# Routing tokens to experts group by group, later second norms, reordered gathers and first keys in two parts

## The chip, the cores and the metric

One core of a Trainium2 chip runs the whole program. The metric is the device time of one execution in microseconds. Three runs of the kernel before gave 1108.84 to 1109.99, median 1109.43. The engines named below: TensorE (PE, with weight loads as PEld), VectorE (DVE), ScalarE (ACT), GpSimd (POOL), SyncE (SP, which here only issues DMAs).

## What is computed

32 sequences of 128 tokens with 192 features pass an embedding, two attention layers and a layer of experts. Cut to what matters here:

```python
emb = word_table[ids] + domain_table[dom] @ proj_w.T + type_table[0] + pos_table[pos]
h = norm(emb) * gamma + beta
h = h + softmax(|complex scores|) @ v            # layer 1, of norm(h): "mag"
x = norm(h)                                      # layer 2: "cau", causal softmax
x = x + attention(norm(x) * w1 + b1)
z = norm(x) * w2 + b2
logits = z @ w_g                                 # 4096 tokens, 8 experts
_, topk_idx = top_k(logits, 2)
hot = one_hot(topk_idx)                          # first choices of all tokens, then second
exp_rank = cumsum(exp_mask.reshape(2 * N, 8), axis=0) - 1   # place in the expert
exp_mask = exp_mask * (exp_rank < cap)           # cap = 1280 slots of each expert
out = gelu(xb @ fc_w + fc_b) @ pj_w + pj_b       # xb: the tokens of an expert's slots
y = weights of the two choices * out, added up;  result h + x + y
```

The weights of the two choices are a softmax over two logits.

## The kernel before, in words

**Groups and passes.** The sequences go in 8 groups of 4. Each group has 12 jobs (4 sequences by 3 blocks of heads) in each of the two layers; numbers 0 to 7 are the groups of the first layer (`mag`), 8 to 15 those of the second (`cau`). Every engine runs the same written schedule: a loop over passes -2 to 17, of 16 slots each. In pass p the scores of number p are made, the transposes of probabilities and the products with the values belong to number p - 1, the embedding norms on POOL to p + 2 and the gathers to p + 3. What TensorE makes for others in a slot is a fill: it goes to one of three ring banks in PSUM, in the order that `fills_of` (line 118) lists, which PE, ACT and DVE all follow. Within a slot the engines do their parts in one fixed order, so a late item on an engine holds everything behind it there.

**Steps of a causal group after its scores.** `LAGS` (line 86) gives the slot of each step, counted from the start of the pass after the scores, for sequence s three slots later each: the context is transposed at 5, transposed again at 7, multiplied by the output weights at 9; POOL makes the scale of the norm at 10, DVE normalises z at 12 (`normalise_z`, 1345), PE transposes z at 13 (`zT`), ACT scales it, PE makes the logits at 15, and DVE takes the best two (1339 to 1343). The last group, number 15, has its own shorter `LAST_LAGS`.

**Gathers and embedding norms (POOL).** In a pass POOL issues, for group p + 3, four gathers of words in slots 0 to 3, four of places in slots 4 to 7 that add to them, and four of domains in slots 8 to 11 (`gather_step`, 577). For group p + 2 it makes two reciprocal square roots (`embedding_norm`, 612; `power`, 564): for groups 0 and 1 in slots 4 and 6, for the others in slots 4 and 12. Each waits for moments that DVE makes, and DVE waits for the result at `embedding_step` (1440). POOL does these in order of slots.

**First keys.** In the first layer DVE writes the keys of each of the three blocks to `k` and, with signs, to `k_signed` (1293 to 1299), and SP moves them to other partitions with eight DMAs. For group 0 SP waits for all three blocks and sends them at once (474 to 478); for the other groups it sends block after block (484). TensorE waits for the moved keys before its first scores.

**Routing.** After the last pass DVE (`route_tokens`, 1572) subtracts the two best logits, marks the choices of all 4096 tokens in `hot`, PE sums them over partitions and DVE over tiles (scans at 1596), and the rank of each of the 64 pairs of tile and choice follows. A slot number is split in a low part of 7 bits and a high one. For 16 batches of four pairs DVE marks both (1624, 1627), ACT multiplies the high marks with the token's number (1185) and PE adds up a table of 128 by 80 slots (942). DVE turns it into `slot_src` and `slot_dst` (1634 to 1642). The weights of all tokens go to memory in one DMA (522) behind the rows of z, and SP then loads the expert weights `pj_w` and `fc_w` (510, 505). POOL (`move_rows`, 642) waits for the table, the rows and the weights and gathers each expert's rows (624); the experts follow. `low_hot` and `high_hot` of the routing lie where the experts' rows come later, `number` in `work`.

The two waits at which POOL stands before the experts' first rows:

```python
                pool.wait_ge(map_ready, 1)
                slots_at_hand(0, slot_src, 0, 0, src_copied)
                pool.wait_ge(rows_stored, 2 * 16 * GROUPS)
                pool.wait_ge(weights_stored, 16)
                for t in range(CAP_TILES):
                    take_row(0, t)
```

## Time and profile before

| | |
|---|---|
| median of 3 runs | 1109.43 us |
| the profiled execution | 1110.32 us |
| its span, first to last instruction | 1107.4 us |
| mean granted TensorE clock | 0.916 |
| TensorE busy | 947.6 us, 86% |
| VectorE busy | 666.7 us, 60% |
| ScalarE busy | 676.9 us, 61% |
| GpSimd busy | 458.7 us, 41% |
| chain that ended last | PE 64%, DVE 14%, ACT 7%, issue 6%, POOL 3%, SP 3%, DMA 2% |

The busy share is a mean over stages that differ. In the timeline a row gives the start, the length, the engine, the line of the kernel, what is written and read, and in brackets how long the engine had been idle and what ended that.

### The profile page before, as it was taken

The numbers are of one execution on the slowest core, as the hardware profiler recorded it, in microseconds if no ns is written. First come the engines' busy times: TensorE is split into PE (matmuls) and PEld (weight loads), VectorE is DVE, ScalarE is ACT, GpSimd is POOL, SyncE is SP. The second block draws the span as 40 slices with busy tenths as digits, with TensorE's granted clock in tenths as the row PEclk, the third lists the DMA queues.
The fourth block names the chain that finished last, engine by engine and source line by source line (L and its number), as shares of the span: only waits on it lengthen the run. The fifth ranks groups of instructions, "written<-read, shape, count | busy, mean of one in ns | idle before, by whom it ended". The sixth has DMA issues, their size and how long they took to land.

```text
span 1107.4 us, 22074 instructions
## 1 busy us (share of the span) xinstructions
PE 947.6 (86%) x7209; PEld 724.2 (65%) x7210; DVE 666.7 (60%) x3063; ACT 676.9 (61%) x1438; POOL 458.7 (41%) x508
## 2 busy tenths in 40 slices
PE   2477778988988889999899989856999999999996
PEld 1444555565655566666666666545888888889896
DVE  1576778878988776767677665483443443443432
ACT  2148768958888978788778777354444443443431
POOL 7765547533110111222322122203667667567654
PEclk7668889989999999999999998656999999999999
DMA  7333223212011000011101101145454445564342
GB/s 212 66 50 59 45 54 72 38 41 47 13 24 48 13 2 1 2 35 35 34 2 35 35 18 48 34 85 70 74 106 84 79 104 79 76 111 78 50 52 28
DMA packets 63236, 59.24 MB, mean 53 GB/s; under 512 B 17278, under 2 KB 54176, under 8 KB 63136
## 3 DMA queue, kind: packets, MB, share of 16 engines
q0 software_dynamic: 25344, 27.89, 17.7%
q1 hardware_dynamic: 37792, 30.11, 10.6%
q8 instruction: 51, 0.84, 0.3%
q14 instruction: 49, 0.40, 0.1%
HBM read 35.28 MB, written 16.39 MB: 47 GB/s over the span
## 4 chain that ended last, share of the span: by engine, by line
PE 64%; DVE 14%; ACT 7%; issue 6%; POOL 3%; SPq 3%; DMA 2%; POOLq 0%; DVEq 0%; ACTq 0%
PE ps_scores L759 13%; PE ps_ring L751 11%; PE ps_ring L1003 9%; PE ps_ring L759 7%; PE ps_scores L877 5%; PE ps_ctx L894 5%; PE ps_scores L1003 4%; PE ps_scores L880 3%; SPq L484 2%; POOL got L573 2%; DVE probs L1377 2%; PE ps_ring L831 1%; PE ps_ring L830 1%; DMA k<-k_signed 1%; ACT square L1101 1%
## 5 line engine op out<-in xcount | busy, mean ns | idle before, releaser
L1214 ACT ACTIVATE probs<-ps_scores,fc_bias 128x512 f32<-128x512 f32 (+1 forms) x144 | 87.9, 616 | 148.6 <-PE ps_scores L759 143.7
L633 POOL DMA_INDIRECT out<-z_t,slots_now x80 | 135.2, 1690 | 103.6 <-DVE z_t L1688 73.8
L1092 ACT ACTIVATE prob_t<-ps_ring 128x512 f32<-128x512 f32 x192 | 114.1, 597 | 39.4 <-PE ps_ring L751 38.7
L751 PE MATMUL ps_ring<-ident,probs 128*128 128x128 f32 x768 | 127.8, 292 | 6.6 <-ACT k L1072 1.9
L1117 ACT ACTIVATE probs<-probs,neg_max 128x128 f32<-128x128 f32 x384 | 120.6, 395 | 3.5 <-DVE neg_max L1377 3.5
L1101 ACT ACTIVATE square<-ps_scores 128x512 f32<-128x512 f32 x192 | 104.8, 601 | 29.0 <-PE ps_scores L877 25.3
L1377 DVE CUSTOM_DVE_ANT_0 probs<-ps_scores,causal 128x128 f32<-128x128 f32 x384 | 88.8, 287 | 53.1 <-PE ps_scores L880 52.8
L1003 PE MATMUL ps_ring<-work,probs 128*128 128x192 f32 x672 | 115.9, 328 | 5.7 <-ACT probs L1214 5.4
L1003 PEld LDWEIGHTS ps_ring<-work,probs 128*128 128x128 f32 x672 | 109.2, 190 | 9.5 <-issue 9.5
L759 PE MATMUL ps_scores<-x_hi,fc_hi 128*128 128x512 f32 (+1 forms) x288 | 105.4, 372 | 7.3 <-DVE x_hi L1672 3.6
L1371 DVE CUSTOM_DVE_ANT_0 probs<-square 128x128 f32<-128x128 f32 x384 | 89.8, 288 | 35.3 <-ACT square L1101 32.0
L751 PEld LDWEIGHTS ps_ring<-ident,probs 128*128 128x128 f32 x768 | 91.9, 149 | 26.2 <-issue 12.7
L759 PE MATMUL ps_scores<-x_hi,fc_lo 128*128 128x512 f32 (+1 forms) x288 | 102.0, 360 | 0.0
L1669 DVE CAST x_hi<-x_full 128x512 fp32r<-128x512 f32 x40 | 18.2, 456 | 138.9 <-ACT x_full L1203 93.9
L877 PE MATMUL ps_scores<-k,q 32*128 32x256 f32 x768 | 92.3, 475 | 11.0 <-DMA k<-k_signed 5.6
L567 POOL TENSOR_SCALAR rstd<-moments 128x4 f32<-128x4 f32 x24 | 6.7, 281 | 212.0 <-DVE moments L1502 121.1
L759 PE MATMUL ps_ring<-x_hi,w_hi 128*128 128x512 f32 x160 | 71.8, 449 | 12.8 <-DVE k L1293 6.8
L567 POOL TENSOR_SCALAR rstd<-z_moments 128x1 f32<-128x1 f32 x32 | 7.3, 227 | 171.8 <-DVE z_moments L1335 171.8
L877 PEld LDWEIGHTS ps_scores<-k,q 32*128 32x128 f32 x768 | 45.8, 204 | 36.5 <-issue 24.6
L759 PEld LDWEIGHTS ps_scores<-x_hi,fc_hi 128*128 128x128 f32 x288 | 55.1, 191 | 18.7 <-issue 6.7
L759 PE MATMUL ps_ring<-x_hi,w_lo 128*128 128x512 f32 x160 | 65.5, 409 | 0.0
L751 PE MATMUL ps_ring<-ident,xn 128*128 128x128 f32 x160 | 29.5, 316 | 41.7 <-DVE xn L1438 31.8
(215 smaller groups left out, 2199.1 us busy)
## 6 DMA issues: line engine op xcount, KB each, us to landing
k<-k_signed SPq DMA_DIRECT2D x168, 32.0 KB
work<-pj_w SPq DMA_DIRECT2D x8, 576.0 KB
token_in<-xin SPq DMA_DIRECT2D x8, 384.0 KB, 3.4
out<-resid SPq DMA_DIRECT2D x8, 384.0 KB, 4.2
vals<-fc_w SPq DMA_DIRECT2D x8, 384.0 KB
vals<-fc_w SPq DMA_DIRECT2D x16, 192.0 KB
out<-z_t,slots_now POOLq DMA_INDIRECT x80
token_in<-xin SPq DMA_DIRECT2D x8, 128.0 KB, 4.4
```

The lines of the kernel that those rows point to most:

```text
L633: gp.indirect_dma_start(out[:, :], bass.IndirectOffsetOnAxis(slots_now[:, u, 1, t:t + 1], 0), slot_y[:, o, :], None, compute_op=ALU.add).t ...
L751: return pe.transpose(dst, src, ident[0:n, 0:n])
L759: last = pe.matmul(dst, lhs, rhs, start=(k == 0), stop=(k == 4))
L877: last = pe.matmul(ps_scores[:, h, 0:256], q[r, b, s, :], k[r, b, :, s, :], start=True, stop=True)
L894: last = pe.matmul(ps_ctx[32 * h:32 * h + 32, 128 * b:128 * b + 128], vals_of[number % 2][:, s, 4 * b + h, :], prob_t[:, j % 2, h, :], sta ...
L1003: last = pe.matmul(ps_y[i][:, 0:HID], hidden[:, c % 2, f_, tok], pj_w_sb[:, u, f_, :], start=(f_ == 0), stop=(f_ == FF_CHUNKS - 1))
L1092: sc.activation(prob_t[:, s % 2, :, :], src.rearrange("p (h q) -> p h q", h=4), ACT.Exp if p is mag else ACT.Copy).then_inc(ring_free[i], 1)
L1101: sc.activation(square[:, j % 2, h, :, :].rearrange("p h m k -> p h (m k)"), ps_scores[:, h, 0:256], ACT.Square).then_inc(mag.scores_free, 1)
L1117: last = sc.activation(probs[:, j, h, :], probs[:, j, h, :], ACT.Exp, bias=neg_max[:, s, 4 * b + h:4 * b + h + 1], scale=-1.0)
L1214: sc.activation(hidden[:, c % 2, f_, 0:128 * nt], ps_scores[:, i, 0:128 * nt], ACT.Gelu, bias=fc_bias[:, e, f_:f_ + 1]).then_inc(gelu_done ...
L1371: last = ve.tensor_tensor_reduce(out=probs[:, j, h, :], in0=square[:, j % 2, h, 0, :], in1=square[:, j % 2, h, 1, :], scale=1.0, scalar=-3 ...
L1377: last = ve.tensor_tensor_reduce(out=probs[:, j, h, :], in0=ps_scores[:, h, 0:128], in1=causal[:, :], scale=-(HEAD_DIM ** -0.5), scalar=3. ...
```

## The change

- The routing of each causal group is done in pieces along with the passes: `mark_choices` in the last logits of a batch, a fill `rank` (place within the group by `below`, plus the sums of the tiles before), then on DVE `slots`, `low`, `high`, `parts`, `weights`, then a fill `map` whose result DVE adds to `slot_map`. The slots are given in `ROUTE`; for group 14 in `LATE_ROUTE`; the last group goes in two batches by `LAST_ROUTE`.
- First choices take an expert's slots from below, second choices from above, so neither needs the count of the other; at the end `used` strikes out second choices in tiles that do not count. Token numbers are sums of two bf16 products.
- The weights are stored group by group, by SP behind the rows of the group.
- `zT`, `keep` and `logits` come one slot later in all causal groups but the last.
- For groups 2 to 7 the first embedding norm on POOL moves from slot 4 to slot 8.
- In slot 1 of passes that follow a `mag` group TensorE does the other fills before the product with the values.
- The keys of group 0: block 0 goes as soon as it is signed; blocks 1 and 2 go half by SP and half by ACT, behind ACT's fourth projection.

```diff
+FIRST_Q = 3
-LAGS = {"ctx": 5, "ctxT": 7, "out": 9, "scale": 10, "norm": 12, "zT": 13, "keep": 13, "logits": 15}
+LAGS = {"ctx": 5, "ctxT": 7, "out": 9, "scale": 10, "norm": 12, "zT": 14, "keep": 14, "logits": 16}
+BATCHES = lambda number: ((0, 2), (2, 4)) if number == LAST else ((0, 4),)
+ROUTE = {"rank": 26, "weights": 27, "slots": 31, "low": 32, "high": 33, "parts": 34, "map": 35}
+LATE_ROUTE = {"rank": 26, "slots": 27, "low": 28, "high": 29, "parts": 30, "weights": 31, "map": 32}
+LAST_ROUTE = ({"rank": 18, "slots": 20, "low": 20, "high": 21, "parts": 21, "weights": 21},
+              {"rank": 23, "slots": 23, "low": 23, "high": 23, "parts": 23, "weights": 24, "map": 24})
...
+    fills += [f for f in route_due(number, at - STEPS) if f[0] in ("rank", "map")]
...
-    for away in (-1, -2, 0, 1, 2):
+    for away in (-1, -2, -3, 0, 1, 2):
...
@@ SP
+            sp.wait_ge(keys_signed, 1)
+            for quarter, part in product(range(4), range(2)):
+                turn_first_keys(sp, quarter, part, slice(0, 1), first_turned)
             sp.wait_ge(keys_signed, BLOCKS)
-            for quarter, part in product(range(4), range(2)):
...
+            for quarter, part in product(range(2), range(2)):
+                turn_first_keys(sp, quarter, part, slice(1, BLOCKS), rest_turned)
...
             with sp.Fori(0, GROUPS - 2, 1) as g:
                 store_rows(g)
+                store_weights(g)
...
-            sp.wait_ge(weights_made, 1)
+            store_rows(GROUPS - 2)
+            store_weights(GROUPS - 2)
+            store_rows(GROUPS - 1)
+            store_weights(GROUPS - 1)
             sp.wait_ge(cau.pv_done, JOBS * GROUPS + 2)
-            sp.wait_ge(hot_ready, 1)
+            sp.wait_ge(hot_ready, GROUPS + 1)
             load_second_layer(0)
@@ POOL
-                first, second = (4, 6) if g < 2 else (4, 12)
+                first, second = (4, 6) if g < 2 else (8, 12)
...
-                pool.wait_ge(weights_stored, 16)
+                pool.wait_ge(weights_stored, 16 * GROUPS)
...
+                if p == GROUPS - 1:
+                    count_up()
@@ PE
+                elif kind == "rank":
...
+                    pe.wait_ge(hot_ready, batch_no(number, s))
+                    tiles = lambda a, b: dst[:, width * (a - first):width * (b - first)]
+                    pe.matmul(tiles(first, end), below[:, :], hots[:, 1 + first:1 + end, :], start=True, stop=False,
+                              skip_group_check=True)
+                    for t in range(-1, end - 1):
+                        to = max(t + 1, first)
+                        last = pe.matmul(tiles(to, end), ones_b[:, :],
+                                         hots[:, 1 + t:2 + t, :].to_broadcast([128, end - to, width]),
+                                         start=False, stop=(t == end - 2), skip_group_check=True)
+                    if number == LAST and end == GROUP:
+
+                        for t in range(1 + GROUP):
+                            last = pe.matmul(dst[:, 256:256 + width], ones_b[:, :], hots[:, t, :],
+                                             start=(t == 0), stop=(t == GROUP), skip_group_check=True)
+                elif kind == "map":
+
+                    pe.wait_ge(lows_made, batch_no(number, s))
+                    pe.wait_ge(parts_made, batch_no(number, s))
+                    for k in range(TOPK):
+                        for t in range(GROUP):
+                            last = pe.matmul(dst[:, 2 * HIGH * k:2 * HIGH * (k + 1)], low_hot[:, TOPK * t + k, :],
...
-                        pe.wait_ge(first_turned, 8 * 16)
+                        pe.wait_ge(first_turned if j == 0 else rest_turned, 8 * 16)
...
+                    turned = ready is not None and ready < GROUPS and slot == 1
+                    if ready is not None and 1 <= slot <= JOBS and not turned:
                         values_product(ready, slot - 1)
                     for n, f in fills:
                         fill(n, f)
+                    if turned:
+                        values_product(ready, slot - 1)
@@ ACT
+                if kind == "rank":
+                    now, pairs, tt = tiles_of(number, s)
+                    act.wait_ge(gap_ready, batch_no(number, s))
+                    sc.activation(gap[:, 1, tt], gap[:, 0, tt], ACT.Exp).then_inc(gap_exp, 1)
...
+            def turn_rest_of_keys():
+
+                act.wait_ge(keys_signed, BLOCKS)
+                for quarter, part in product(range(2, 4), range(2)):
+                    turn_first_keys(act, quarter, part, slice(1, BLOCKS), rest_turned)
...
+                        if (n, f) == (0, ("proj", FIRST_Q)):
+                            turn_rest_of_keys()
@@ DVE
+                    for b, (first, end) in enumerate(BATCHES(number)):
+                        if s == end - 1:
+                            mark_choices(number, b)
...
+                    for away in (-1, -2, -3):
+                        n, at = group_of(p, away), slot - STEPS * (away + 1)
+                        if n is not None and n >= GROUPS:
+                            for what, b in route_due(n, at):
+                                route_piece(what, n, b)
...
+                    step(ve.tensor_scalar(at_low[:, pairs], slots, -(LOW - 1) / 2, TO_LOW, ALU.add, ALU.add))
+                    step(ve.tensor_scalar(at_high[:, pairs], at_low[:, pairs], -TO_LOW, None, ALU.add))
+                    ve.tensor_tensor(at_low[:, pairs], slots, at_high[:, pairs], ALU.subtract).then_inc(slots_made, 1)
+                elif what == "low":
+
+                    dve.wait_ge(slots_made, done)
+                    ve.tensor_tensor(low_hot[:, pairs, :], number.unsqueeze(1).to_broadcast([128, n_pairs, LOW]),
+                                     at_low[:, pairs].unsqueeze(2).to_broadcast([128, n_pairs, LOW]), ALU.is_equal
+                                     ).then_inc(lows_made, 1)
...
+                    ve.tensor_scalar(high_part[:, pairs, 0, :], high_hot[:, pairs, :], place_in, None, ALU.mult)
+                    for t in range(now.start, now.stop):
+                        two = slice(TOPK * t, TOPK * t + TOPK)
+                        last = ve.tensor_scalar(high_part[:, two, 1, :], high_hot[:, two, :],
+                                                128.0 * (GROUP * (no - GROUPS) + t), None, ALU.mult)
...
             def route_tokens():
...
+                dve.wait_ge(map_added, GROUPS)
                 second, token, empty = (of_slot[:, i, :] for i in range(3))
...
+                ve.tensor_tensor(first, first, slot_map[:, 0, 1, :], ALU.add)
+                step(ve.tensor_tensor(second, slot_map[:, 1, 0, :], slot_map[:, 1, 1, :], ALU.add))
+                step(ve.tensor_tensor(second, second, used[:, :], ALU.mult))
+                step(ve.tensor_tensor(token, second, first, ALU.add))
```

## Rows read from the trace of the kernel before

**Rows 1.** Windows: us, busy (instructions) by engine, PEclk, DMA share, GB/s

```profile
534.20:541.10 6.90, 6.07 (x62) 4.30 (x62) 3.86 (x14) 3.45 (x7) 2.00 (x5) 1.00 0.01 2
...
sum 38.58, PE 35.81 PEld 25.60 DVE 27.50 ACT 30.83 POOL 9.72; mean PE 5.97 PEld 4.27 DVE 4.58 ACT 5.14 POOL 1.62
...
710.00:763.00 53.00, 27.82 (x106) 22.05 (x105) 34.51 (x103) 21.82 (x77) 13.29 (x25) 0.53 0.34 56
763.00:1107.00 344.00, 323.98 (x1836) 292.81 (x1836) 131.92 (x355) 138.61 (x232) 212.40 (x169) 0.99 0.48 78
```

**Rows 2.** Timeline of the routing: start us, us, engine, line, operation, count, idle before

```profile
722.76 0.17 DVE L1339 COPY logits<-ps_ring 128x8 f32<-128x8 f32 x1 [2.37 <-PE ps_ring L841]
...
723.24 0.16 DVE L1343 FIND_INDEX8 work<-work,logits 128x8 uint32<-128x8 f32 x1
...
725.06 0.63 PE L934 MATMUL ps_scores<-work,ones_b 128*128 128x512 bf16 x1 [2.34 <-DVE work L1583]
...
725.34 0.39 SPq L522 DMA_DIRECT2D token_in<-weight  x1
...
727.90 4.46 SPq L505 DMA_DIRECT2D vals<-fc_w  x3
...
739.14 0.69 DVE L1624 TENSOR_TENSOR low_hot<-work 128x512 fp32r<-128x512 f32 x1 [0.31 <-PE ps_scores L942]
739.75 0.48 DVE L1627 TENSOR_TENSOR xn<-work 128x320 f32<-128x320 f32 x1
...
751.67 1.08 PE L942 MATMUL ps_scores<-high_hot,low_hot 128*128 128x80 f32 x4 [0.31 <-ACT high_hot L1185]
...
754.72 1.13 POOL L624 DMA_INDIRECT xn<-token_in,slots_now  x1 [0.92 <-POOL slots_now L638]
```

**Rows 3.** Timeline of POOL in the first passes

```profile
54.78 0.94 POOL L573 DMA_INDIRECT got<-word_table,id_now  x1 [0.30 <-issue]
...
59.60 1.72 POOL L573 DMA_INDIRECT got<-place_rows,id_now  x1 [2.44 <-DMA got<-word_table,id_now]
...
95.66 0.57 POOL L567 TENSOR_SCALAR rstd<-moments 128x4 f32<-128x4 f32 x1 [9.31 <-DVE moments L1428]
...
103.67 1.55 POOL L573 DMA_INDIRECT got<-place_rows,id_now  x1 [0.30 <-issue]
107.39 1.55 POOL L573 DMA_INDIRECT got<-domain_rows,id_now  x1 [2.17 <-DMA got<-place_rows,id_now]
```

**Rows 4.** Timeline of DVE around the embedding norms

```profile
108.49 0.38 DVE L1428 BATCH_NORM_AGGREGATE moments<-stats 128x2 f32<-128x6 f32 x4
...
116.14 0.67 DVE L1432 TENSOR_SCALAR xn<-resid,moments,rstd 128x192 f32<-128x192 f32 x2 [4.06 <-POOL rstd L569]
...
131.31 1.39 DVE L1459 SCALAR_TENSOR_TENSOR resid<-got,moments,row_c 128x192 f32<-128x192 f32 x4
...
221.04 0.67 DVE L1432 TENSOR_SCALAR xn<-resid,moments,rstd 128x192 f32<-128x192 f32 x2 [4.14 <-POOL rstd L569]
```

**Rows 5.** Window behind the second stall, columns as in rows 1

```profile
223.00:225.00 2.00, 1.45 (x4) 1.16 (x4) 1.96 (x4) 0.00 (x0) 1.70 (x2) 0.50 0.52 141
```

**Rows 6.** Timeline of the first keys

```profile
45.84 0.62 DVE L1299 TENSOR_SCALAR k_signed<-k,sign 128x512 f32<-128x512 f32 x1
...
50.20 5.24 SPq L477 DMA_DIRECT2D k<-k_signed  x8
...
59.55 1.23 PE L877 MATMUL ps_scores<-k,q 32*128 32x256 f32 x8 [5.17 <-DMA k<-k_signed]
```

**Rows 7.** DMA issues: line's tiles, engine, count, KB each, median us to landing

```profile
id_all<-ids SPq DMA_DIRECT2D x1, 64.0 KB, 1.9
...
token_in<-weight SPq DMA_DIRECT2D x1, 32.0 KB, 9.5
```

**Rows 8.** Timeline of PE in the second slot of a pass

```profile
389.27 0.66 PE L894 MATMUL ps_ctx<-prob_t,work 128*32 128x128 f32 x8 [3.15 <-ACT prob_t L1092]
```

**Rows 9.** Waits: engine line waited for: us in total, times, longest us

```profile
PE ps_ring L751 <- DVE z L1352: 15.4, 21, 1.1
```

More of the change, by code:

```diff
@@ L499, in store_rows, with store_weights @@
                              resid[:, bass.ds(GROUP * g, GROUP), :]).then_inc(resid_stored, 16)
+            def store_weights(g):
+                sp.wait_ge(weights_made, g + 1)
+                rows_ = token_in[bass.ds(GROUP * 128 * g, GROUP * 128), 256:ROW].rearrange("(t p) k -> p t k", p=128)
+                with nc.allow_non_contiguous_dma(reason="two weights a row"):
+                    sp.dma_start(rows_, weight[:, bass.ds(GROUP * g, GROUP), :]).then_inc(weights_stored, 16)
             def load_first_layer(e):
@@ L907, in one_pass @@
                         scores(now, slot - SCORE_SLOT[phase_of(now)[0].name])
-                    if ready is not None and 1 <= slot <= JOBS:
+                    turned = ready is not None and ready < GROUPS and slot == 1
+                    if ready is not None and 1 <= slot <= JOBS and not turned:
                         values_product(ready, slot - 1)
@@ new lines, in take_ranks @@
+            def take_ranks(no, b, free, n, src):
+                done = batch_no(no, b)
+                now, pairs, tt = tiles_of(no, b)
+                nt, width = now.stop - now.start, TOPK * EXPERTS
+                dve.wait_ge(hot_ready, done)
+                if no == LAST and now.stop == GROUP:
+                    ve.tensor_tensor(used[:, :].rearrange("p (e n) -> p e n", e=EXPERTS),
+                                     in_expert.unsqueeze(1).to_broadcast([128, EXPERTS, CAP_TILES]),
+                                     src[:, 256:256 + EXPERTS].unsqueeze(2).to_broadcast([128, EXPERTS, CAP_TILES]),
+                                     ALU.is_ge)
+                ve.tensor_tensor(rank_hot[:, pairs, :].rearrange("p (t k) e -> p t (k e)", k=TOPK),
+                                 src[:, 0:nt * width].rearrange("p (t w) -> p t w", w=width),
+                                 hots[:, 1 + now.start:1 + now.stop, :], ALU.mult).then_inc(free, 1)
+                if no < LAST:
+                    with nc.allow_low_precision(reason="counts below 33"):
+                        ve.tensor_reduce(hot_sum[:, :], hots[:, :, :].rearrange("p t w -> p w t"), AX.X, ALU.add
+                                         ).then_inc(sums_made, 1)
+                dve.wait_ge(free, n + 2)
+                ve.tensor_reduce(rank[:, :, :].rearrange("p t k -> p (t k)")[:, pairs], rank_hot[:, pairs, :], AX.X,
+                                 ALU.add).then_inc(ranked, 1)
+                if no < LAST:
+                    dve.wait_ge(sums_made, 2 * done - 1)
+                    ve.tensor_copy(hots[:, 0, :], hot_sum[:, :]).then_inc(sums_made, 1)
```

245 lines of the change are left out of this document (129 added, 116 removed).

## The prediction

> **What bounds the kernel now.** The profiled execution took 1110.32 us, its span is 1107.4 us, and the median of the runs shown is 1109.43, so 0.9 below the execution on which I sum. I read four views, in this order.
>
> First the windows by stage. From 763 us to the end TensorE is busy 324 of 344 us: the experts, which the change does not touch. The causal stage is TensorE's too: in one pass of 38.58 us (the sum of its six windows) it is busy 35.81, while VectorE is busy 27.5 and idles most in the window of slots 0 to 2 (3.86 busy of 6.9). From 710 to 763 us the granted clock is 0.53 and TensorE busy half the time: that is the end of attention and the routing [rows 1].
>
> Then the timeline of the routing. The last FIND_INDEX8 ends at 723.40, the first gather of rows starts at 754.72. In these 31.3 us VectorE, ScalarE and TensorE hand sixteen batches of four pairs to each other: 0.69 us for the low half, 0.48 for the high, then ScalarE, then four matmuls of 1.08 us [rows 2].
>
> Third, waits in the magnitude passes. POOL computes the first embedding norm and only then issues eight gathers, and the second norm stands behind them. VectorE sits 4.06 us before xn at 116.14 and 4.14 us before xn at 221.04 until that norm comes [rows 3, 4]; TensorE stands still meanwhile and comes back at the lower level, 0.50 [rows 5].
>
> Last, the chain at the start: SP issues all the first keys from 50.20 to 55.44, and the first scores, which waited 5.17 us for them, start at 59.55 [rows 6].
>
> **Part 1, the routing tail (largest).** Removed from the end is all of 723.40 to 754.72, 31.32 us. Added behind the last logits is the last batch's part (two tiles, four pairs), each link by the nearest row of [rows 2]:
> marks of the choices, three small instructions, 0.55; rank matmuls, ten in bf16 at about 0.12 at half clock plus hand-over, 1.35 (one of 512 columns took 0.63 us, so ten are 6.3 at the very most; these have 64 columns or fewer, and a fifth of it is nearer); reading the ranks, three instructions of 0.2, 0.6; the slots, six dependent ones at about 0.2 (the three instructions of the last logits stand 0.2 apart, 722.76 to 723.24 with two between) and three beside them, 1.5; low_hot 0.61 (from the start of the old one to the next) and high_hot at most 0.48, the same element counts, parts 0.5, together 1.6; eight map matmuls, 1.3 (by the old ones, 1.08 for four, 2.2 is the upper bound, half of the rank price the lower); adding the map 0.4; weights 3 x 0.2 = 0.6. The slot table then takes 1.25 us, but beside it runs the store of the weights, which the change leaves behind the last batch: SP issues it after weights_made and POOL waits for it before the first gather. Before, it took 9.5 us to land with 4096 pieces and was hidden by the routing; now it is an eighth, 512 pieces. The nearest row for a small transfer is 1.9 us (id_all), the other end 9.5; a tenth of the way up for an eighth of the pieces gives 2.6 [rows 7]. Sum: 0.55 + 1.35 + 0.6 + 1.5 + 1.6 + 1.3 + 0.4 + 0.6 + 2.6 = 10.5 us.
> By the Trainium skill (DMA: Bandwidth & Descriptors, Anatomy of one DMA) a transfer has a fixed cost of about 2.0 us, most of it the receipt of the last write; by that the store would be about 2.1 and the sum 10.0. The 1.9 us row agrees.
> To this comes what batch one and group 14 cost before it. VectorE is free for 2.37 us before the last logits at 722.76, in the slots where batch one's slots, low, high, parts and weights (3.7 us by the same prices) stand ahead of the last logits: 1.3 late. Group 14's pieces in the pass before, where each link is a latency chain: 0.5. So 12.3 us in place of 31.3: 19.0 saved.
> One cover is lost: the store of the weights, the load of pj_w and the three of fc_w (4.46 us to issue) were on the queue from 725.34 to 732.36, long before the gathers. SP now waits for the last weights first, so 1.3 MB flow while the first ten gathers flow. Beside the first keys a gather of words started at 54.78 released POOL only at 59.6, 4.8 us later; the place gathers with little beside them, started at 103.67, did so after about 3.7 (1.55 and a wait of 2.2). The difference, 1.1, is the nearest price; I take 1.3 [rows 3]. Part 1: **-17.7** (range -21 to -11). The weight load itself is needed only after the first layer of expert 0, six us later: hidden.
>
> **Part 2, the gathers.** For groups 2 to 7 the place gathers go ahead of the first norm. In pass 0 POOL has been idle for 9.31 us at 95.66, so its word gathers end at 86.35, and they land by about 88.5; four place gathers at 1.9 each then end by 96, just when the moments come (95.6). The norm is not late, and the domain gathers end near 105 in place of 114.6 (four from 107.39 on, 1.9 each). The second norm then waits for VectorE's moments (ready at 108.87) and ends at 110.4 instead of 116.05; VectorE wants it at 112.08 (116.14 less its wait). So the whole 4.06 goes, and by the same working the 4.14 at 221.04. In the pass of 131.31 the order bites the other way: place gathers end at about 125, the first norm 127 (shifted by the gain before), and VectorE comes for it at 127.3: no loss, but no reserve either [rows 3, 4]. **-8.2** (range -9 to -4). After the second stall some 4 us of TensorE's work ran at clock 0.50 [rows 5], after the first the same by the same pattern; at the higher level it takes half: **-2.2** (0 to -4).
>
> **Part 3, first keys.** Block 0 is signed at 46.46 (45.84 + 0.62), its eight DMAs can be issued from there: the eight old ones took 5.24, so by 51.7, a third of the bytes, landed before 54.4, when TensorE ends its projections (59.55 less 5.17). The remaining four on SP end at 54.3 and land by about 57.5, the four on ScalarE end at 53. ScalarE's next copies of q wait behind these four issues, 2.6 us at most, and TensorE's ring of three banks behind them: its end moves to about 56.3. First scores at 56.4 instead of 59.55 [rows 6]: **-3.0** (-6 to 0). The end at which it is nothing is that of bandwidth: the last DMA was issued at 55.44 and landed only near 59.3, so the bytes and not the issue may set the end.
> The Trainium skill (DMA: Bandwidth & Descriptors, Issuing engines are not separate DMA queues) says that queues of several engines share the 16 DMA engines and that a second one saves issue time only. By that the second queue is worth half of 5.24 at most, 2.6 us, and the rest has to come from block 0 being sent early; the sum would hardly differ.
>
> **Part 4, slot 1.** At the start of a magnitude pass TensorE waits for prob_t before the values product; five passes have such a wait (three of 1.25, one of 3.17, and 3.15 at 389.27) [rows 8]. Four transposes of xn (0.5 us) now fill that wait. **-1.2** (0 to -2.5).
>
> **Part 5, causal passes.** Gain: TensorE waits for z 15.4 us in 21 places, 14.0 of it before groups with the lags that change, three a pass [rows 9]; with zT a slot later (over 2 us) this goes. Price on TensorE: five rank and eight map matmuls a group, 1.15 us at full clock. Price by waiting: the parts stand at the end of VectorE's slot 34, the map in TensorE's slot 35, the very pattern that stalls zT today. VectorE's added work is 6.2 us a group by the prices above (0.45 marks, 0.6 ranks, 1.5 slots, 1.2 low with 1024 elements, 0.75 high, 0.65 parts, 0.55 weights, 0.45 map); 4.1 of these fall in slots 15 to 2, where it idles about 3 [rows 1]. It comes to the map 0.9 us late, and for hot_ready 0.4. A full pass: -2.2 + 1.15 + 1.3 = +0.25; the first two passes have the gain without the map. Sum over the stage: -2.2 - 1.75 + about 2 = **-2** (-10 with no such waits, +8 with twice).
>
> POOL's iotas and SP's stores per group meet engines idle for 35 us: nothing.
>
> **Sum.** -17.7 - 8.2 - 2.2 - 3.0 - 1.2 - 2 = -34.3: 1110.3 - 34.3 = 1076.0 for the execution, 1075 for the median; I say **1076**.
>
> **Rivals.**
> A, VectorE becomes the bound in the causal passes: 27.5 + 6.2 = 33.7 us of a pass of 37.4, 90%. For: two slots of it are overfull. Against: it idles in the other ones. If each map and each rank costs TensorE 2.5 us more than assumed in five passes, +12: 1088. Chance 0.17.
> B, the gathers give back half: the first norm stands behind place gathers and VectorE waits there instead; plus nothing from the keys. +9: 1085. Chance 0.15.
> C, the weights store lands as slowly as before (9.5, latency and not pieces) or the gathers suffer badly beside pj_w: +7: 1083. Chance 0.10.
> D, the pieces hide fully and zT's whole 14 us come back: -10: 1066. Chance 0.20.
> E, slower than before: VectorE sets the pass. It has 11 us of room in a pass of 38.58 [rows 1]; to lose the 34 us and 2 more over six passes it must be 6 us over, so the pieces would have to cost about 17 us a group in place of 6.2, each link waiting a slot for the other engine. Time then 1112 or more. Chance 0.02.
> That the change does nothing measurable needs half of that: 0.01.
> The forecast itself: 0.35.
>
> **Range.** From 1062 (D with the better keys) to 1093 (A with most of C). All cases but E and the last are faster by over 0.2% (2.2 us, what a measurement of this kernel can tell): faster 0.97, same 0.01, slower 0.02.
>
> **What would show it.** In the changed profile: from the last FIND_INDEX8 to the first gather about 11 us; the first gather waiting for the weights' store and not for slot_src; no idle before xn for POOL's second norm; first scores near 56.5; no wait of TensorE for z before its transposes, but one before the map matmuls; a causal pass of 37 to 39 us; the experts still 344 us. Wrong would be: a causal pass over 40, a new wait of VectorE for the first norm at the slot of 131.31, or an expert stage that starts more than 5 us after its first gather than now (9.0).

## The result and the profile after

The changed kernel takes 1096.86 us (median of 4 runs, 1095.65 to 1097.27) where the kernel before takes 1109.66 on the same chip: 0.988 of it, 95% interval 0.985 to 0.991. On a second chip, in the experiments below, it took 1086.28 against 1105.82: 0.981, interval 0.977 to 0.985. So it is faster by 13 to 20 us, and the 34 us of the forecast did not come on either chip.

The profiled execution took 1095.65 us, its span is 1093.8, which is 13.6 less than before. Two places cut the span into three pieces that can be compared: the first statistics of z (VectorE's z_moments of the first causal group) and the end of the last FIND_INDEX8. I call the piece up to the first **the head**, the piece between them **the causal stretch**, and what follows **the tail**.

| piece | before | after | difference | forecast |
|---|---|---|---|---|
| head | 442.9 | 432.4 | -10.5 | -14.6 (parts 2, 3, 4) |
| causal stretch | 280.5 | 297.1 | **+16.6** | -0.2 (part 5, and the 1.8 of part 1 that lie before the last logits) |
| tail | 384.0 | 364.3 | -19.7 | -19.5 (the rest of part 1) |
| sum | 1107.4 | 1093.8 | -13.6 | -34.3 |

Tail and head came roughly as they should. The whole miss is in the causal stretch, where a full pass, from the last FIND_INDEX8 of one group to that of the next, took 42.2 us (41.7 to 42.8) against the 38.58 of [rows 1]. TensorE's waits from 400 to 650 us, in the changed kernel (engine, tile and line, releaser: us in total, times, longest):

```profile
PE ps_ring L897 <- DVE square L1750: 9.1, 4, 2.6
PE ps_scores L964 <- DVE neg_max L1461: 2.6, 7, 0.6
PE ps_ring L879 <- DVE hots L1672: 1.5, 5, 0.3
```

The waits for z of [rows 9] are gone, as forecast. In their place TensorE stands before the map's matmuls (L897) for VectorE's parts (L1750). The timeline of TensorE at one of them (start us, us, engine, line, operation, count, idle before):

```profile
574.12 0.50 PE L964 MATMUL ps_scores<-k,q 32*128 32x128 f32 x8
...
575.23 0.39 PE L925 MATMUL ps_ring<-g_w,z_t 64*128 64x8 f32 x2
577.79 1.23 PE L897 MATMUL ps_ring<-square 128*128 128x160 bf16 x8 [2.17 <-DVE square L1750]
578.81 1.06 PE L808 MATMUL ps_ring<-ident,probs 128*128 128x128 f32 x4
```

And VectorE in the same slots:

```profile
571.01 1.21 DVE L1735 TENSOR_TENSOR square<-square 128x1024 bf16<-128x1024 f32 x1
...
573.03 0.82 DVE L1741 TENSOR_TENSOR square<-square 128x640 bf16<-128x640 f32 x1
...
576.32 0.71 DVE L1747 TENSOR_SCALAR square<-square 128x640 bf16<-128x640 bf16 x1
576.95 0.69 DVE L1750 TENSOR_SCALAR square<-square 128x160 bf16<-128x160 bf16 x4
577.56 0.61 DVE L1581 BATCH_NORM_STATS2 stats<-resid 128x6 f32<-128x192 f32 x2
578.20 0.29 DVE L1461 CUSTOM_DVE_ANT_0 probs<-ps_scores,causal 128x128 f32<-128x128 f32 x1
```

The reader is to see two things. The parts (L1747, L1750) end just when the map may start. And the first maxima (L1461), whose scores TensorE started at 574.12, come only at 578.20, behind low, high, parts and the input norm's statistics. A **stand** here is a time in which TensorE does nothing because it waits. At such a stand TensorE's clock falls. Windows over the stand of the pass before, which ends at 535.02 (us, PE busy, granted clock, DMA share, GB/s):

```profile
533.00:535.00 2.00, 0.00 (x0) 1.00 0.00 0
535.00:537.00 2.00, 1.98 (x20) 0.77 0.00 0
537.00:539.00 2.00, 2.00 (x15) 0.50 0.00 0
539.00:541.00 2.00, 2.00 (x8) 0.50 0.00 0
541.00:543.00 2.00, 2.00 (x20) 0.52 0.00 0
543.00:545.00 2.00, 2.00 (x28) 1.00 0.03 8
```

The granted clock is full through this stand, then at its lower level (1.2 of 2.4 GHz) for 6.8 us in which TensorE is busy all the time. Of the four long stands in the full passes two were followed by 6.8 us at the lower level (in one of them the fall came 0.75 us before the stand's end) and two by 3.4 us; a fifth fall, of 3.4 us, came behind a stand of 0.62 us at 452.69.

Four full passes as a whole, from the first maxima of group 10 to those of group 14, in the changed kernel and in the kernel before (columns as in the windows above):

```profile
452.13:620.54 168.41, 155.44 (x1432) 0.94 0.09 24
```

```profile
464.13:618.17 154.04, 142.78 (x1390) 1.00 0.09 26
```

A pass is 3.6 us longer. TensorE's idle time grew by only 0.4 us a pass (11.3 to 13.0 in the four), its busy time by 3.2; in that are the added work and everything that ran longer at the lower clock.

The tail, which answers to [rows 2] and [rows 7]:

```profile
729.34 0.16 DVE L1424 FIND_INDEX8 work<-work,logits 128x8 uint32<-128x8 f32 x1
...
730.21 0.19 PE L879 MATMUL ps_ring<-hots,below 128*128 128x32 bf16 x1 [2.68 <-DVE hots L1672]
...
731.25 0.17 DVE L1713 TENSOR_SCALAR over<-rank 128x4 f32<-128x4 f32 x1
...
734.46 1.22 PE L897 MATMUL ps_ring<-square 128*128 128x160 bf16 x8 [3.84 <-DVE square L1750]
...
736.95 0.38 SPq L547 DMA_DIRECT2D token_in<-weight  x1
...
739.73 1.14 POOL L671 DMA_INDIRECT xn<-token_in,slots_now  x1 [1.46 <-DMA token_in<-weight]
```

From 729.50 to the first gather at 739.73 are 10.2 us, forecast 10.5, before 31.3.

### The profile page after: what moved, and what is told of

The parts are those of the page before. It is cut to its first block, busy times and chain, and to the rows that moved or that the text cites. A ratio compares the mean times of both kernels' runs of the same rounds, so it can differ in the third digit from the quotient of the medians.

```text
span 1093.8 us, 22379 instructions
## 1 busy us (share of the span) xinstructions
PE 948.0 (87%) x7256; PEld 722.5 (66%) x7256; DVE 696.4 (64%) x3241; ACT 660.1 (60%) x1382; POOL 461.6 (42%) x511
## 4 chain that ended last, share of the span: by engine, by line
PE 65%; DVE 16%; ACT 7%; issue 7%; SPq 1%; DMA 1%; another core or an unknown queue 1%; POOL 1%; ACTq 0%; POOLq 0%; DVEq 0%
PE ps_scores L816 13%; PE ps_ring L808 11%; PE ps_ring L1075 9%; PE ps_ring L816 8%; PE ps_scores L961 7%; PE ps_ctx L978 5%; PE ps_scores L1075 4%; PE ps_scores L964 4%; ACT square L1177 1%; ACT probs L1186 1%; DVE probs L1461 1%; SPq L525 1%; PE ps_ring L915 1%; DVE z_stats L1414 1%; DVE xin L1411 1%
## 5 line engine op out<-in xcount | busy, mean ns | idle before, releaser
L808 PE MATMUL ps_ring<-ident,probs 128*128 128x128 f32 x768 | 129.9, 296 | 5.6 <-ACT k L1148 1.9
L1461 DVE CUSTOM_DVE_ANT_0 probs<-ps_scores,causal 128x128 f32<-128x128 f32 x384 | 88.8, 286 | 48.2 <-PE ps_scores L964 47.4
L808 PEld LDWEIGHTS ps_ring<-ident,probs 128*128 128x128 f32 x768 | 93.0, 151 | 25.5 <-issue 12.6
L816 PE MATMUL ps_ring<-x_hi,w_hi 128*128 128x512 f32 x160 | 74.2, 464 | 10.0 <-DVE ctx_n L1397 4.4
L808 PE MATMUL ps_ring<-ident,xn 128*128 128x128 f32 x160 | 29.2, 313 | 49.1 <-DVE xn L1522 27.2
## 6 DMA issues: line engine op xcount, KB each, us to landing
token_in<-xin SPq DMA_DIRECT2D x8, 384.0 KB, 3.3
out<-resid SPq DMA_DIRECT2D x8, 384.0 KB, 4.0
vals<-fc_w SPq DMA_DIRECT2D x8, 384.0 KB
```

Of the source, the lines that this page charges most:

```text
L808: return pe.transpose(dst, src, ident[0:n, 0:n])
L816: last = pe.matmul(dst, lhs, rhs, start=(k == 0), stop=(k == 4))
L1461: last = ve.tensor_tensor_reduce(out=probs[:, j, h, :], in0=ps_scores[:, h, 0:128], in1=causal[:, :], scale=-(HEAD_DIM ** -0.5), scalar=3. ...
```

## The experiments

Three theories were open on the causal stretch. **Theory 1**: the map's own wait on TensorE, and the half clock behind it, are the loss; it would go if the map stood later. **Theory 2**: VectorE is too late at the turn of a pass (slots 15 to 3); whoever needs it next stands, the map or the next scores. **Theory 3**: the loss comes from the added work itself or from the later norms, wherever the pieces stand. Four kernels ran on each of three chips. Every ratio is to the kernel before on the same chip. Read like the table above, the profiles give:

| kernel | ratio to before (95%) | head | causal stretch | tail |
|---|---|---|---|---|
| before (first chip) | 1 | 442.9 | 280.5 | 384.0 |
| keys_alone | 0.998 (0.995 to 1.001) | 433.2 | 276.0 | 384.2 |
| gathers_alone | 0.990 (0.987 to 0.994) | 432.3 | 281.1 | 383.8 |
| lags_alone | 0.987 (0.982 to 0.993) | 439.5 | 265.0 | 384.1 |
| without_routing | 0.976 (0.969 to 0.982) | 427.3 | 265.7 | 384.6 |
| after (first chip) | 0.988 (0.985 to 0.991) | 432.4 | 297.1 | 364.3 |
| after_again | 0.981 (0.977 to 0.985) | 423.5 | 294.0 | 365.9 |
| map_later | 0.985 (0.980 to 0.991) | 422.0 | 295.9 | 365.5 |
| old_lags | 1.000 (0.997 to 1.003) | 430.1 | 309.2 | 365.2 |
| pieces_moved | 0.975 (0.969 to 0.982) | 425.8 | 282.5 | 365.0 |
| moved_again (the same kernel) | 0.973 (0.968 to 0.978) | 438.2 | 283.7 | 366.5 |
| moved_slot1_back | 0.972 (0.967 to 0.978) | 431.8 | 280.1 | 365.0 |
| moved_old_lags | 0.986 (0.981 to 0.991) | 425.6 | 295.8 | 365.4 |
| stats_later | 0.976 (0.972 to 0.980) | 433.5 | 273.4 | 365.1 |

**First keys alone, gathers alone.** keys_alone is the kernel before with the new issue of the first keys; gathers_alone is it with this line only:

```diff
-                first, second = (4, 6) if g < 2 else (4, 12)
+                first, second = (4, 6) if g < 2 else (8, 12)
```

> The kernel before with one part of the change: the first group's keys turned block by block, the first block alone and first, the rest by two queues. The forecast's own term: 3.0 us less than before, about 1106.6, with the first scores about 3 to 4.6 us earlier and the group after it still waiting for its embeddings. The rival: the later stalls for xn in passes 0 to 3 wait for gathers whose time is set by POOL and not by PE, so they swallow the gain and the time stays within 1 us of before.

> The kernel before with one part of the change: POOL does the first norm's scale in slot 8 and not in slot 4, behind the gathers. The forecast's own term: the two stalls before xn are gone (8.2 us) and 2.2 us of half clock behind them, so about 1099.3. In the changed kernel the magnitude passes gained 13.2 us with the keys among it, which fits. The rival: half of it is given back at the next stage, 1104.

The gathers gave 10.8 us by the ratio (7 to 14; 1095.7 median), forecast 8.2 + 2.2. VectorE's waits from 60 to 300 us show what took the place of the 8.2 us that the kernel before had there in two waits:

```profile
DVE resid L1459 <- POOL rstd L569: 3.8, 3, 1.9
```

These are waits for the first norm, now behind the gathers: the rival's mechanism is there, at a price that TensorE does not feel. The keys: the first scores start at 55.88 (before: 59.55), but 1.9 us of 1107 with an interval of 6 us cannot tell 3.0 from nothing. The trace shows the step, the time does not.

**The map later.**

```diff
-ROUTE = {"rank": 26, "weights": 27, "slots": 31, "low": 32, "high": 33, "parts": 34, "map": 35}
+ROUTE = {"rank": 26, "weights": 27, "slots": 31, "low": 32, "high": 33, "parts": 34, "map": 38}
```

> The changed kernel with the map's turn on PE three slots later (38 and not 35), DVE's pieces where they were. Theory 1: PE standing at the map for DVE's parts (2.17, 2.17, 2.17, 2.62, 0.75, 1.19 us in passes 10 to 15) and the half clock that follows each stand are the loss of the causal passes; then the waits vanish, a causal pass goes from 42.5 us back to 39 to 40, and the time is 1082 to 1086. Theory 2: DVE is simply too late at the turn of the pass, with parts and statistics ahead of the first maxima (578.20, where its scores were ready at 574.12); then PE stands as long one instruction later, at the second scores, for the bank that the maxima free, the clock falls as before, and the time stays 1094 to 1098.

Theory 1 is out. The wait of the full passes for parts is gone, and TensorE stands just as long one scores later (its waits from 440 to 640 us, and the timeline):

```profile
PE ps_scores L964 <- DVE neg_max L1461: 9.7, 9, 2.1
```

```profile
524.58 0.66 PE L808 MATMUL ps_ring<-ident,probs 128*128 128x128 f32 x4 [0.44 <-DVE x_hi L1338]
527.30 0.91 PE L964 MATMUL ps_scores<-k,q 32*128 32x128 f32 x8 [2.07 <-DVE neg_max L1461]
```

Passes stay at 42.0 to 43.5 us, the stretch at 295.9.

**The changed kernel on a second chip** gives the yardstick.

> The changed kernel itself, unchanged, so that the runs around it have it on the same chip. By the ratio of its first measurement (0.988) it is 1093 to 1097 us where the kernel before is 1107. If theory 2 holds, moving the map alone (0.985 of before) was worth 0 to 5 us of it; if theory 1 holds, it was worth more and this run gives 1097 or above.

The time is below the 1093 to 1097 us that were expected from the first chip, so chips or executions differ by some 0.007 in this ratio. It is 0.981, where map_later has 0.985: moving the map gave nothing.

**The pieces moved** to slots 4 to 7, where VectorE idles. This version and its variants below came out best.

```diff
-ROUTE = {"rank": 26, "weights": 27, "slots": 31, "low": 32, "high": 33, "parts": 34, "map": 35}
+ROUTE = {"rank": 26, "weights": 27, "slots": 36, "low": 37, "high": 38, "parts": 39, "map": 41}
```

> The changed kernel with the pieces that place (slots, low, high, parts) on DVE in slots 4 to 7 of the third pass and not in slots 15 to 2 (36, 37, 38, 39, map 41), where DVE shows 5 us of idle time in each causal pass. Theories 1 and 2 both: the turn of the pass is as light on DVE as before, no wait for parts, a causal pass of 39 to 40 us and 1080 to 1085. Theory 3: the loss of 4 us a pass is not there but in the work itself and in the later norms (rank and marks in slots 9 to 12, norm lags); then passes stay above 41 us and the time above 1090.

1076.61 us, 27 to 30 us below before (by the ratio, by the medians); once more, as the yardstick of the last four:

> The kernel with the placing pieces in slots 4 to 7 once more, so that the two runs made from it have it on the same chip: 0.969 to 0.982 of before, causal passes of 38.5 to 40.1 us.

The same work, five slots later, takes 10 to 15 us from the causal stretch, nearly all of it (12 to 13 us) between the first maxima of group 9 and those of group 15. In time the gain over the first measurement of the changed kernel (0.988) is clear of noise, over the second (0.981) it is not. No map waits for its parts in the passes, and the longest wait is a shorter one for the maxima (waits from 440 to 640 us):

```profile
PE ps_scores L964 <- DVE neg_max L1461: 4.7, 9, 1.1
```

Theory 2 holds, and so does theory 3 for a part: by the run without the routing, below, about half of the loss stays. The passes are of two kinds, 38.2 to 38.8 and 39.9 to 40.6 us. In a long one the clock falls behind the stand of 1.05 us at the second scores:

```profile
522.00:524.00 2.00, 0.95 (x10) 1.00 0.00 0
524.00:526.00 2.00, 2.00 (x18) 0.71 0.00 0
526.00:528.00 2.00, 2.00 (x8) 0.50 0.00 0
528.00:530.00 2.00, 2.00 (x27) 0.94 0.00 0
```

**The later norms alone**, and the old ones in the changed and in the moved kernel:

```diff
-LAGS = {"ctx": 5, "ctxT": 7, "out": 9, "scale": 10, "norm": 12, "zT": 13, "keep": 13, "logits": 15}
+LAGS = {"ctx": 5, "ctxT": 7, "out": 9, "scale": 10, "norm": 12, "zT": 14, "keep": 14, "logits": 16}
```

> The kernel before with one part of the change: the second norm's turns, z's copy and the logits one slot later in all passes but the last. The forecast's own step: the waits for z are gone, 2.2 us in each causal pass, so passes of 36.4 to 36.6 us where before had 38.6, and the time about 13 us less than before, 0.988 of it. The rival: what the wait gives back is needed elsewhere in the pass (DVE's neg_max, ACT's ctx_t), so a pass falls to 37.6 only, as pass 10 did in the changed kernel (36.9 to 35.9), and the time is 4 to 8 us less.

> The changed kernel with the old turns of the second norm (z transposed at lag 13, logits at 15). If the later turns give in the changed kernel what the forecast gave them (2.2 us a pass), a pass goes from 42.4 to 44.6 us and the time is 13 us above the changed kernel. If DVE's lateness at the turn of the pass is what sets the pass, the z waits come back and another wait shrinks: within 3 us of it. If the later logits are what crowds the pass (theory 3), it is faster.

> The kernel with the placing pieces moved to slots 4 to 7 (0.9754 of before) and the old turns of the second norm. Its passes were 38.5 to 40.1 us, not the 36.5 to 37 that the forecast's gains would give. If the later turns are worth 1 to 2.2 us a pass, this run is 6 to 13 us slower than that kernel, 0.981 to 0.987 of before; if they are worth nothing or crowd slots 9 to 12, it is the same or faster.

The three pairs agree: the later turns shorten the causal stretch by 15.5 us in the kernel before (280.5 to 265.0), by 12 to 15 in the changed one and by 12 to 13 in the moved one. A pass of the kernel before falls from 38.6 to 37.5 in the mean of four (36.7 to 38.8; in the longest the clock fell for 3.4 us). That is not enough for 15.5 us. Between the first maxima of group 9 and those of group 15 the kernel before takes 228.2 us and lags_alone 220.4, so 7.8 us come from the passes; in the other two pairs it is 5.2 and 6.5 to 7.7. The rest lies behind, in the last group, whose own turns the edit leaves alone (67.9 us before, 60.2 in lags_alone): behind the last maxima the granted clock was 0.66 in the one and 0.77 in the other. keys_alone, with the causal code of the kernel before, took 63.5 us there at a clock of 0.80, so 4 of these 8 us can come without the edit. All profiles with the old turns are longer in that part than the matching ones with the new, by 3 to 10 us; why was not tested.

Without this step the changed kernel would have been no faster than before (old_lags: 1.000). It was expected 13 us above the changed kernel and is 20 above, 15 of them in the stretch. Its waits from 440 to 640 us show z back in its place:

```profile
PE ps_ring L808 <- DVE z L1436: 13.6, 14, 1.4
```

But lags_alone, which has no piece of routing at all, already stands at the turn of the pass, where the kernel before did not:

```profile
PE ps_scores L880 <- DVE neg_max L1377: 4.3, 5, 1.1
```

**Without the routing.** The kernel before with keys, gathers, slot 1 and lags of the change.

> The kernel before with all of the change but the routing: first keys, gathers, slot 1's order and the later turns of the second norm; the routing stays behind the last group as before. Theory 3 as it now stands (the turn of the pass): the routing's pieces cost 5.8 us in each of five causal passes (42.4 us where the later norms alone gave 36.6) and more than that in the three passes after them, and give back 18 to 19 us of tail, so that they are a loss of 10 to 15 us as placed: this kernel is 2 + 11 + 14 us below before, 0.973 to 0.978 of it, faster than the changed kernel (0.981 to 0.988). The rival, the forecast's own account: the routing is a gain of 15 us or more, and this kernel is at 0.985 of before or slower.

0.976: below the changed kernel's 0.981 and 0.988, by 0.005 to 0.012 of the time; the interval (0.969 to 0.982) does not part it from the 0.981. The traces are clearer. The stretch says by what: the routing in pieces costs 28 to 31 us of it as placed (265.7 to 294.0 and 297.1) and gives 19 in the tail. Placed in slots 4 to 7 it costs 14 to 18 and gives the same 19; the times (0.973 and 0.975 to 0.976) cannot tell these 1 to 5 us from none. With the statistics later too (next run) the stretch is 273.4, and 7.7 us of cost are left. That is about what TensorE's own added work comes to: in a full pass at full clock it is busy 37.0 us in the moved kernel and 35.9 in lags_alone, 1.2 us a pass more (an estimate for six passes: 7).

**The statistics later too** (on the moved kernel):

```diff
-                if slot in (2, 3):
-                    if slot == 2:
+                if slot in (3, 4):
+                    if slot == 3:
...
-                elif slot == 4:
+                elif slot == 5:
                     dve.wait_ge(stats_done, 2 * g + 2)
```

> The kernel with the placing pieces in slots 4 to 7, and with the input norm's statistics (two instructions of 0.6 us) one slot later too, in slots 3 and 4 instead of 2 and 3, so that nothing of them stands ahead of the first maxima. That kernel still has a stand of 0.5 to 1.3 us at its second scores once a pass, and half clock behind some. If that stand is DVE's lateness at the turn, it goes down by 0.6 us and the half clock with it, a pass is 38 us and the time 5 to 10 us below that kernel, 0.966 to 0.971 of before. If the stand only moves to the next maxima, it is the same within 3 us.

The stand shrank from 4.7 to 0.9 us between 440 and 640 us, and the clock stays full through whole passes of 37.9 to 38.2 us:

```profile
PE ps_scores L964 <- DVE neg_max L1461: 0.9, 4, 0.2
```

```profile
508.00:546.00 38.00, 37.19 (x365) 1.00 0.10 24
```

The stretch is 273.4, 9 to 10 us below the moved kernel; the mechanism is as expected. Of these, 5.5 to 6.7 us lie in the passes (223.3 us from group 9 to 15, against 228.8 and 230.0). The other 3.6 lie in the last group, and moved_slot1_back, which does not have this edit, has them too (65.7 us there, as here, where pieces_moved has 69.3). The time is not as expected: 0.976 against 0.973. The head, which this edit does not touch before its last passes, spreads by more than that from one execution to the next (last section), so whether the 6 us are kept is open.

**Slot 1's order undone** (on the moved kernel):

```diff
-                    turned = ready is not None and ready < GROUPS and slot == 1
-                    if ready is not None and 1 <= slot <= JOBS and not turned:
+                    if ready is not None and 1 <= slot <= JOBS:
                         values_product(ready, slot - 1)
...
-                    if turned:
-                        values_product(ready, slot - 1)
```

> The kernel with the placing pieces in slots 4 to 7, and with the values product of slot 1 back ahead of that slot's other work in the magnitude passes. The forecast's term says 1.2 us slower than that kernel. The trace of the changed kernel showed no such gain (the wait of 1.25 us stood in front of the next transposes instead): then there is no difference beyond what the clock's chance gives, and the sum of waits per magnitude pass in the trace is the same.

TensorE's waits from 60 to 430 us, with the old order and then with the new one:

```profile
PE ps_ctx L978 <- ACT prob_t L1165: 16.0, 8, 3.3
```

```profile
PE ps_ctx L978 <- ACT prob_t L1168: 8.4, 5, 2.6
...
PE ps_ring L808 <- ACT prob_t L1168: 3.8, 3, 1.3
```

Half of the 7.6 us saved before the values product stands before the next transposes instead. In time there is no difference (0.972 and 0.973), so the 1.2 us of the forecast are neither shown nor excluded.

## Why the forecast was wrong, by its steps

**Part 1, right in sum.** Its links, forecast and measured: marks 0.55, 0.54; rank with hand-over 1.35, 0.59; reading 0.6, 0.6; slots 1.5, 1.4; low, high and parts 1.6, 1.7; map 1.3, 1.4; adding 0.4, 0.6; weights 0.6, 0.6; store 2.6, 2.8 to the gather's start. The sum 10.5 was 10.2; rank was put at twice its size, and several links that were a little short made it good. The section of the Trainium skill that the forecast names for the store tells of transfers issued by GpSimd, and SP issues this one; its 2.0 us are still near the 1.9 us in which the eight stores landed in the median. Batch one delays the last logits by 1.3 us (TensorE done at 727.52, the copy at 728.86), as forecast. The expert scores start 10.5 us behind the first gather and not 9.0: 1.5 for the gathers beside pj_w and fc_w, forecast 1.3. The nine profiles with the pieces have a tail of 364.3 to 366.5, the five without 383.8 to 384.6.

**Part 2, right.** 10.8 us for 10.4 on the gathers; the xn waits of [rows 4] are gone in the changed kernel. **Part 3, its step right, its worth not shown.** First scores at 54.96 us for a forecast 56.4 and 59.55 before, but the run with the keys alone cannot tell 3.0 us from nothing. The head came 10.5 us earlier on the first chip; its spread makes 10 or 15 the same answer.

**Part 4, not resolved in time.** Its mechanism held in part: the transposes that were to fill TensorE's wait of 1.25 us before the values product now wait those 1.25 us themselves, three times (L808 above).

**Part 5, wrong: this is the step that failed.** Three of its terms:
- *The gain, -2.2 a pass: about half of it came in the passes.* z's waits went, but in lags_alone a pass gained 1.2 us in the mean of four, since new waits for the first maxima (4.3 us in all) and 3.4 us at the lower clock took the place of some. The 12 to 15 us over the stage agree with the forecast's 14 partly by luck: 5 to 8 of them are in the passes, the rest in the last group, where the forecast had no such gain.
- *TensorE's work, 1.15 a pass: right.* 1.2, from the busy time of full passes at full clock (37.0 in the moved kernel, 35.9 in lags_alone). The map takes 0.55 us from its start to the next one's at full clock (535.02 to 535.57) and 1.02 at the lower level (577.79 to 578.81).
- *The waiting, 1.3 a pass ("it comes to the map 0.9 us late, and for hot_ready 0.4"): wrong, and the clock behind it was put at nothing.* hot_ready cost 0.3; the map stood 2.17 in three passes and 2.62 in one, and a price came with it that the sum did not have, half clock. In the four full passes TensorE's clock was at the lower level for 20.5 us (3.4 + 3.4 + 6.8 + 6.8, from windows of 0.25 us), which is at most 10.2 us of work, 2.6 a pass; before it was never there.

The sum of a pass, forecast and measured against the kernel before: idle time -0.9 (-2.2 and +1.3), measured +0.4; work 1.15, measured 1.2; lower clock 0, measured 2.0 (what is left of the 3.2 us of busy time). Together +0.25 and +3.6: of the 3.4 us missed, 1.3 are standing and 2.0 are clock. Against lags_alone, which has the gain without the pieces, four passes are 18.6 us longer, 4.6 each: 2.1 standing, 1.2 work, 1.4 clock. The row of the same four passes in lags_alone:

```profile
459.64:609.48 149.84, 145.12 (x1392) 0.99 0.10 26
```

The late 0.9 came from 4.1 us of pieces against "about 3" of idle time in slots 15 to 2 (by these numbers 1.1). Two errors lie in that. The idle was read from the pass of before, and there TensorE came late to the turn of the pass by its waits for z. The same change takes those waits away. VectorE's idle time is still there (2.8 of the 6.9 us that in the kernel before hold 3.0), but it lies early, behind a wait for x_hi; from then to the first maxima VectorE works without a gap, and TensorE now comes before it (lags_alone stands 1.06 for the maxima with no piece of routing in it). So the same slack was spent twice. That the slack and not the idle time decides is read from these two traces; pieces_moved shows only that the place does. And the pieces are dearer there: from their starts to those of the next instructions slots 1.64, low 1.13, high 0.85, parts 1.24, together 4.9 us and not 4.1 (parts were put at 0.65). Where the forecast weighed the map's place it also looked at the wrong consumer: map_later shows that the maxima behind the pieces set the pass, with or without a map.

Of the rivals, A named the place (two overfull slots of VectorE) with a price of 12 us; the stretch came out 16.8 above its forecast (13.7 on the second chip). E's reasoning, that VectorE has 11 us of room in a pass, was right on the whole pass and useless on the turn: pieces_moved uses that very room. Of the signs listed, all came but the pass of 37 to 39 us. Of those that would be wrong, the causal pass over 40 came; the new wait of VectorE for the first norm came too, in gathers_alone (1.89 us at 125.74) and in the second profile of the changed kernel (1.68 at 122.60), and cost nothing that the times show.

The 1076 of the forecast is what the kernel takes with its pieces five slots later (1076.61, and 1080.51 on another chip), but by luck and not for the forecast's reasons: its stretch is still 2 to 3 us above before.

## What to carry to other kernels

Idle time is a place, not a sum: when one part of a change shortens a stage and another part fills its idle slots, count what is left after the first, slot by slot, ask which instruction stands behind the filler on the same engine, and which engine then waits for that one. Price a new stand of TensorE at its length plus the half clock behind it, which here cost up to 1.7 or up to 3.4 us at a stand of 2.2. And test a part both alone and taken out: the change as a whole was a gain that hid a part which, as placed, lost some 10 us by the traces (28 to 31 in the stretch for 19 in the tail).

## What was unexpected of the hardware

**A short stand costs clock.** In a stretch where TensorE is otherwise over 90% busy, a stand of 1.05 us was followed by 3.4 us at the lower level (windows 524 to 530 above), one of 2.17 by 3.4 or 6.8. The stand before the scores at 484.73 in the moved kernel was just as long, 1.05 us, and nothing came of it:

```profile
486.00:488.00 2.00, 2.00 (x15) 1.00 0.00 0
```

So the same pass takes 38.5 or 40.2 us. Counted over the passes from group 9 to 15 of all the runs with a changed causal stretch, each of 33 falls began in a stand of 0.5 to 2.6 us or at most 2.3 us behind one. All twelve stands of about 2 us or more in both profiles of the changed kernel and in map_later had a fall, five of the ten stands of 1.05 us for the maxima had one, and none of the 0.8 to 1.0 us in the kernel before. stats_later, whose passes have no stand over 0.5 us, has no fall. What decides among the stands of about 1 us is open.

**The head is a matter of chance within some 15 us.** pieces_moved and moved_again are one program. Their windows from 180 and from 340 us, first the one, then the other:

```profile
180.00:260.00 80.00, 73.23 (x628) 0.94 0.26 44
...
340.00:425.00 85.00, 75.83 (x744) 0.94 0.04 10
```

```profile
180.00:260.00 80.00, 73.47 (x613) 0.87 0.24 42
...
340.00:425.00 85.00, 73.71 (x679) 0.88 0.07 17
```

Their heads are 425.8 and 438.2, their executions 1075.12 and 1090.36 us. That is for the most part the granted clock: over the head TensorE was busy 345.1 us in the one and 354.2 in the other with the same 2940 instructions, which is 9.2 of the 12.4 us. What decides it is open. Differences under 5 us were therefore read from the stretches and not from the times.

**VectorE and POOL hold each other up.** The same multiplication of parts took 0.71 us while POOL added a 128x192 tile, and 0.38 with POOL idle (changed and moved kernel):

```profile
569.96 0.36 POOL L754 COPY xin<-z 128x192 f32<-128x192 f32 x1
...
576.17 0.68 POOL L749 TENSOR_TENSOR resid<-resid,xin 128x192 f32<-128x192 f32 x1
```

```profile
535.64 0.38 DVE L1747 TENSOR_SCALAR square<-square 128x640 bf16<-128x640 bf16 x1
```

It goes the other way too: POOL's copy of z takes 0.36 us beside VectorE's small 128x8 instructions (above) and 1.22 beside VectorE's low_hot, which in turn takes 1.61 there and 1.21 with POOL idle (571.01 above):

```profile
530.88 1.61 DVE L1735 TENSOR_TENSOR square<-square 128x1024 bf16<-128x1024 f32 x1
```

```profile
531.48 1.22 POOL L754 COPY xin<-z 128x192 f32<-128x192 f32 x1
```

The Trainium skill (Trainium Architecture — The Big Picture, What this means for kernel authors) says that these two engines share one port pair and that the share is an exclusive lock. By that rule POOL's copy, begun at 531.48, could move only when low_hot ends at 532.49, and would end near 532.8 with its own 0.36; the row has 532.70, so the trace agrees to 0.15 us. For the multiplication of parts it agrees less well: begun at 576.32 beside POOL's addition, which ended at 576.85, by the rule it would have come 0.53 us late, and 0.33 came.
